# Router and norm of both chunks of the first batch moved into the last attention stage, with five smaller changes

## The reference

```python
x = L0_attn_x                                   # (2, 1024, 128), fp32
x = _layernorm(x + attn(x, qw, kw, vw, ow))     # 16 heads of 8, rope, causal softmax
x = _layernorm(x + ffn(x, router_w, router_b, w1, w3, w2))
# ffn: logits = x @ router_w + router_b ; the best 2 of 4 experts, their probabilities
#      normalised to sum 1 are the gates; expert e: (silu(x @ w1[e]) * (x @ w3[e])) @ w2[e],
#      w1, w3: (4, 128, 512), w2: (4, 512, 128); out = sum of gates * expert
```

## Time and profile before

| | us |
|---|---|
| median of 3 runs | 436.62 (435.84 to 437.49) |
| profiled execution, its time | 432.75 |
| its span | 430.7 |
| busy: PE, DVE, ACT, POOL | 391.1, 315.1, 265.1, 193.5 |
| mean granted TensorE clock | 0.955 |

### The profile page before, as it was taken

One profiled execution on the slowest core, in us unless ns is written; L12 is line 12 of the kernel. 1 busy time (PEld: TensorE's weight loads), 2 busy tenths in 40 slices (PEclk: granted clock), 3 DMA queues, 4 the chain that ended last, 5 costly groups with the idle time before them and its releaser, 6 DMA issues.

```text
span 430.7 us, 7532 instructions
## 1 busy us (share of the span) xinstructions
PE 391.1 (91%) x2420; PEld 202.9 (47%) x2420; DVE 315.1 (73%) x1027; ACT 265.1 (62%) x377; POOL 193.5 (45%) x256
## 2 busy tenths in 40 slices
PE   4658769999999999999999888999999999999991
PEld 2243122232323323233232331788887887888770
DVE  3659888999999999999999543346576658656653
ACT  1233615687786867778687886566665656665550
POOL 7627611261343515235261322466565646655661
PEclk9959686999999999999999998999999999999996
DMA  6474841322213122131210000000000000000000
GB/s 216 153 203 91 286 115 23 75 53 57 52 22 89 39 70 51 25 93 22 74 35 3 1 3 2 0 2 1 2 1 24 2 1 24 2 1 3 24 0 24
DMA packets 45244, 21.13 MB, mean 49 GB/s; under 512 B 30995, under 2 KB 42899, under 8 KB 45206
## 3 DMA queue, kind: packets, MB, share of 16 engines
q1 hardware_dynamic: 44950, 20.47, 18.2%
q10 hardware_dynamic: 256, 0.20, 0.2%
HBM read 13.11 MB, written 7.35 MB: 47 GB/s over the span
## 4 chain that ended last, share of the span: by engine, by line
PE 70%; DVE 9%; ACT 5%; DMA 4%; issue 4%; POOL 3%; SPq 3%; ACTq 0%; POOLq 0%; DVEq 0%
PE o_bank L1127 14%; PE t_bank L1195 9%; PE bank L1084 9%; PE bank L1195 9%; PE t_bank L1206 9%; PE t_bank L1109 8%; PE small_bank L1084 5%; DMA q_op<-max_rows 3%; SPq L442 3%; ACT num L696 2%; DVE num L912 2%; POOL roped L509 1%; DVE num L985 1%; DVE x_w L850 1%; PE o_bank L1214 1%
## 5 line engine op out<-in xcount | busy, mean ns | idle before, releaser
L696 ACT ACTIVATE num<-t_bank 128x1024 f32<-128x1024 f32 (+2 forms) x160 | 142.8, 939 | 60.4 <-PE t_bank L1109 59.7
L610 POOL TENSOR_TENSOR hid_lo<-num,q_op 128x512 fp32r<-128x512 f32 x64 | 83.0, 1300 | 61.2 <-ACT q_op L749 60.0
L574 POOL TENSOR_SCALAR_AFFINE_SELECT num<-num 128x512 f32<-128x512 f32 x64 | 40.1, 636 | 120.7 <-ACT num L696 120.7
L1084 PE MATMUL bank<-k_op,q_op 128*128 128x512 bf16 (+7 forms) x256 | 71.8, 339 | 11.4 <-DMA q_op<-q_scratch 7.1
L1127 PE MATMUL o_bank<-num,v_op 128*32 128x512 f32 (+3 forms) x768 | 81.5, 503 | 0.1
L749 ACT ACTIVATE q_op<-num 128x512 fp32r<-128x512 f32 x64 | 40.5, 632 | 45.0 <-DVE num L985 44.5
L854 DVE TENSOR_REDUCE maxima<-bank 128x1 f32<-128x512 f32 x86 | 57.0, 684 | 2.6 <-PE bank L1084 1.6
L1109 PE MATMUL t_bank<-q_op,k_op 64*128 64x512 bf16 (+3 forms) x384 | 49.6, 337 | 4.3 <-ACTq L677 1.7
L1084 PEld LDWEIGHTS bank<-k_op,q_op 128*128 128x128 bf16 x256 | 21.2, 99 | 63.6 <-DVE maxima L854 23.4
L985 DVE TENSOR_TENSOR num<-bank,num 128x512 f32<-128x512 f32 x32 | 22.1, 691 | 30.7 <-ACT num L756 30.5
L850 DVE CUSTOM_DVE_ANT_0 mg_w<-bank,resid 128x256 f32<-128x256 f32 (+7 forms) x92 | 39.3, 447 | 4.7 <-PE bank L1084 3.8
(11 more groups left out here) (142 smaller groups left out, 629.2 us busy)
## 6 DMA issues: line engine op xcount, KB each, us to landing
q_op<-q_scratch SPq DMA_DIRECT2D x64, 48.0 KB
w_raw<-in_w_all SPq DMA_DIRECT2D x6, 512.0 KB, 4.0
k_op<-k_scratch SPq DMA_DIRECT2D x60, 48.0 KB, 1.9
xT<-in_x_feat SPq DMA_DIRECT2D x4, 256.0 KB, 5.9
q_op<-max_rows SPq DMA_DIRECT2D x64, 3.0 KB
out_tokens<-num SPq DMA_DIRECT2D x4, 256.0 KB, 2.3
q_scratch<-num SPq DMA_DIRECT2D x2, 384.0 KB, 2.8
k_scratch<-num SPq DMA_DIRECT2D x2, 384.0 KB, 2.8
```

The costliest lines, as they stand in the source:

```text
L574: pool.affine_select(out=tile, in_=tile, compare_op=ALU.is_ge, fill=0.0, base=0, pattern=[[0, GH], [1, P]], channel_multiplier=-1)\
L610: pool.tensor_tensor(hid_lo[:, m % HB, :], hid[:, m % HB, :], hid_hi[:, m % HB, :].bitcast(F32), ALU.subtract).then_inc(f_lo, 1)
L696: act.activation(num[:, t % PB, :, off:CH].rearrange("p (k i) t -> p i k t", i=2)[:, :, h:h + each, :], t_bank[k % TB][:, :, 0:each * (CH ...
L1084: ins = pe.matmul(ring(s, step)[:, i * width:(i + 1) * width], q_op[u][:, pr, j, :, :].rearrange("p i q -> p (i q)"), k_op[u][:, pr, lo:lo ...
```

## The change

- **C steps of two chunks in LAST.** There are 22 slots instead of 15; slot i holds r = i of chunk 0 and r = i - 7 of chunk 1. C_AT, the T units behind which they stand, is now 2, 2, 3, 4, 5, 6, 6, 7, 8, 9, 10, 10, 11, ..., 19. Chunk 1 uses PSUM bank 1, chunk 0 bank 0 as before. In these steps the copies of r = 0, 1, 7 and 8 are VectorE's, the store of x1 (r = 9) is GpSimd's, and ScalarE keeps only the tanh. The slots 0 and 1 stand ahead of MROWS(1) in the list, where slot 0 alone stood. Each chunk has its own chain semaphore. Between the experts of chunks 0 and 1 nothing is left of `between`.
- **Experts ahead of the last NORM.** The units 0 and 1 of TensorE's experts stand between the last OCOPY and the last NORM, and wait for the top two of both chunks. The other engines' order is as it was.
- **Rope.** For n = 0 and 1 sum and third part are VectorE's; for n = 4 to 7 the first rest is GpSimd's, inside its P step. Table 0 is loaded by ScalarE's queue.
- **FIRST** has its own string: MROWS(1) behind four S units instead of two, a NORM (of the ones that o_sb[1] is filled with) early, the T units further apart.
- **W2** takes the two products with the high part first and waits for the low part only ahead of the third.
- **C_AT_UNIT** spreads the steps of chunks 2 and 3 over the units: r = 0 at unit 0, nothing at unit 1, r = 1, 2, 3 at units 2, 3, 4, r = 5 to 14 at units 5 to 14.

```diff
@@ -80,7 +80,14 @@
 C_STEPS = 15
-C_AT = [2 + 16 * r // 14 for r in range(C_STEPS)]
+C_LAG = 7
+C_SLOTS = C_STEPS + C_LAG * (NC - 1)
+C_AT = [2 + 17 * i // (C_SLOTS - 1) for i in range(C_SLOTS)]
+def c_steps_of(slot):
+    return [(ch, slot - C_LAG * ch) for ch in range(NC) if 0 <= slot - C_LAG * ch < C_STEPS]
...
         plan.append(("T", c, kt, h, ahead))
-        if not with_s and at in C_AT:
-            plan.append(("C", C_AT.index(at)))
+        plan += [("C", i) for i in range(C_SLOTS) if C_AT[i] == at]
         part = min(1, t_work(t_units[S_LATE:x + 1]) / max(1, t_work(t_units[S_LATE:len(t_units) - S_EARLY])))
         while done_s < len(s_units) and s_work(s_units[:done_s + 1]) <= part * s_work(s_units):
...
                 plan += pv(t)
-        plan.append(("NORM", NC - 1))
+        plan += [("E", 0), ("E", 1), ("NORM", NC - 1)]
...
 STEADY_ORDER = "ssmttssspssttsspssttsspsstspsttssspmsttsssptsspssttssspssttsspssttsspsnttnpp"
+FIRST_ORDER = "ssssmssssnsssststsstsstsssttsspssttsspmsttssspssttsspssttsspssnttppp"
...
 assert [sum(x[0] == k for x in STEADY) for k in ("S", "T", "PV", "MROWS", "NORM")] == [NS, NT, NPV, 2, 2]
-FIRST = steady_plan(STEADY_ORDER.replace("t", "", SEG_T[0] - T_END[0]).replace("p", "", TI), done=TI - 1)
+FIRST = steady_plan(FIRST_ORDER, done=TI - 1)
...
 HEAD = Z_STEP + 1 - UNITS
+C_AT_UNIT = [0, C_STEPS, 1, 2, 3, *range(5, C_STEPS), C_STEPS]
...
+        def load_table(eng, c):
+            cols = slice(c * CH, (c + 1) * CH)
+            eng.dma_start(cos_sb[:, cols], cos_t[:, cols]).then_inc(ld_tab[c], 16)
+            eng.dma_start(sin_sb[:, cols], sin_t[:, cols]).then_inc(ld_tab[c], 16)
         def load_q(eng, n, u, c, heads):
...
                 sp.dma_start(xT[:, ch * CH:(ch + 1) * CH], x_feat[:, ch * CH:(ch + 1) * CH]).then_inc(ld_x[ch], 16)
-                if ch < NC:
-                    cols = slice(ch * CH, (ch + 1) * CH)
-                    sp.dma_start(cos_sb[:, cols], cos_t[:, cols]).then_inc(ld_tab[ch], 16)
-                    sp.dma_start(sin_sb[:, cols], sin_t[:, cols]).then_inc(ld_tab[ch], 16)
+                if ch == 1:
+                    load_table(sp, 1)
...
+            def first_rest(n):
+                pool.wait_ge(part_ready[0], n + 1)
+                pool.tensor_tensor(roped[:, n % 2, :], roped[:, n % 2, :], rope_part(n, 0), ALU.subtract)\
+                    .then_inc(rest_ready, 1)
             def sum_of_turns(n):
                 pool.wait_ge(turned, n + 1)
...
             pool.memset(minus_half[:, :], -0.5).then_inc(ops_filled, 1)
-            sum_of_turns(0)
-            sum_of_turns(1)
             def lay_v(g, b, u):
...
                             third_part(step[1] - 1)
+                        if step[1] < 2 * CHUNKS:
+                            first_rest(step[1])
                     if 0 <= n < GROUPS - 1 and step == ("T", 1, 1, 0, 0):
                         pool.wait_ge(pv_done, PB + NPV * n)
                         lay_v((n + 1) % NG, (n + 1) // NG, u)
                     if step[0] == "C":
-                        between(0, step[1], first=True)
+                        for ch, r in c_steps_of(step[1]):
+                            between(ch, r, first=True)
                     if step[0] != "T":
                         continue
...
-            third_part(0)
-            third_part(1)
             for n in range(2, PROJ_FIRST):
                 sum_of_turns(n)
...
+                if first and r == 9:
+                    pool.wait_ge(c_x1, 1 + ch + 1)
+                    pool.tensor_copy(x1[:, ch * TI:(ch + 1) * TI, :].rearrange("p i d -> p (i d)"), x1_w[:, :])\
+                        .then_inc(c_store, 1)
                 if r == 3:
                     pool.wait_ge(c_var, ch + 1)
...
                     experts(i, n)
-                    between(i + 1, n - HEAD)
+                    if i + 1 >= NC:
+                        between(i + 1, C_AT_UNIT[n - HEAD])
             for n in range(HEAD, Z_STEP + 1):
                 experts(CHUNKS - 1, n)
...
+            load_table(act, 0)
             act.wait_ge(ld_proj, 32)
...
                     if step[0] == "C":
-                        between(0, 0, 0, step[1], first=True)
+                        for ch, r in c_steps_of(step[1]):
+                            if r == 12:
+                                between(ch, 0, ch, r)
             for n in range(-1, GROUPS - 1):
                 stage(STAGES[n + 1], n, split=n > 0)
-            def between(ch, b, c, r, first=False):
-                turns = bank[0] if first else bank[7]
+            def between(ch, b, c, r):
+                turns = bank[7]
                 if r == 0:
-                    act.wait_ge(job_read, SB + (LAST_JOBS if first else NJOBS))
+                    act.wait_ge(job_read, SB + NJOBS)
                     act.wait_ge(c_mgt, 1 + ch)
                     act.activation(mg_w[:, :].rearrange("p (i g r) -> p i g r", i=TI, g=NG),
...
+            def sum_of_turns(n):
+                dve.wait_ge(turned, n + 1)
+                dve.tensor_tensor(roped[:, n % 2, :], by_cos[:, n % 2, :], by_sin[:, n % 2, :], ALU.add)\
+                    .then_inc(roped_ready, 1)
+            def third_part(n):
+                dve.wait_ge(part_ready[1], n + 1)
+                dve.tensor_tensor(rope_part(n, 2), roped[:, n % 2, :], rope_part(n, 1), ALU.subtract)\
+                    .then_inc(part_ready[2], 1)
             turns_of(0)
-            for n in range(1, PROJ_FIRST):
+            sum_of_turns(0)
+            turns_of(1)
+            first_rest(0)
+            sum_of_turns(1)
+            third_part(0)
+            first_rest(1)
+            third_part(1)
+            for n in range(2, PROJ_FIRST):
                 turns_of(n)
-                first_rest(n - 1)
+                if n > 2:
+                    first_rest(n - 1)
             first_rest(PROJ_FIRST - 1)
...
                             turns_of(step[1])
-                        if step[1] > PROJ_FIRST:
-                            first_rest(step[1] - 1)
                     if step[0] == "MROWS":
                         _, c, use = step
...
                     if step[0] == "C":
-                        between(0, step[1], first=True)
+                        for ch, r in c_steps_of(step[1]):
+                            between(ch, r, first=True)
             CHAIN_0, CHAIN = 0, NC
...
-                C_CHAIN = 1 + 2 * TI + 12
-                turns = bank[0] if first else bank[7]
+                turns = bank[ch] if first else bank[7]
                 def then(ins, k):
-                    ins.then_inc(c_step, 1)
-                    dve.wait_ge(c_step, ch * C_CHAIN + k)
+                    ins.then_inc(c_step[ch], 1)
+                    dve.wait_ge(c_step[ch], k)
                 k = 1 + 2 * TI
+                if first and r == 0:
+                    dve.wait_ge(job_read, SB + LAST_JOBS)
+                    dve.wait_ge(c_mgt, 1 + ch)
+                    dve.tensor_copy(mg_w[:, :].rearrange("p (i g r) -> p i g r", i=TI, g=NG),
+                                    merged[:, 1:1 + NG, ch * TI:(ch + 1) * TI, :].rearrange("p g i r -> p i g r")).then_inc(c_mg, 1)
+                if first and r == 1:
+                    dve.wait_ge(c_mgt, 1 + ch + 1)
+                    dve.wait_ge(c_y, 1 + ch)
+                    dve.tensor_copy(mg_t[:, :], turns[:, :]).then_inc(c_mgs, 1)
                 if r == 1:
                     dve.wait_ge(c_y, 1 + ch + 1)
                     then(dve.tensor_tensor(resid[:, :], turns[:, :],
                                            x_res[:, bass.ds(ch * TI, TI), :].rearrange("p i d -> p (i d)"), ALU.add), 1)
                 if r == 2:
-                    statistics(lambda i: resid[:, i * D:(i + 1) * D], c_step)
+                    statistics(lambda i: resid[:, i * D:(i + 1) * D], c_step[ch])
                 if r == 3:
-                    variance(c_step, ch * C_CHAIN + 1, c_var)
+                    variance(c_step[ch], 1, c_var)
                 if r == 5:
                     dve.wait_ge(c_x1t, 1 + ch)
                     dve.wait_ge(c_store, 1 + ch)
                     dve.wait_ge(c_rstd, ch + 1)
                     normalise(lambda i: resid[:, i * D:(i + 1) * D], lambda i: x1_w[:, i * D:(i + 1) * D], c_x1)
+                if first and r == 7:
+                    dve.wait_ge(c_x1t, 1 + ch + 1)
+                    dve.tensor_copy(x1_hi[ch], turns[:, :]).then_inc(c_hi, 1)
                 if r == 7:
                     dve.wait_ge(c_hi, 1 + ch + 1)
                     dve.tensor_tensor(x1_lo[ch], turns[:, :],
@@ -946,6 +998,10 @@
                 upper = tri[:, 0:1, :].broadcast_to([P, TI, E * E])
                 lower = tri[:, 1:2, :].broadcast_to([P, TI, E * E])
                 gt_f, ge_f = (m[:, :, :, :].rearrange("p i e j -> p i (e j)") for m in (gt, ge))
+                if first and r == 8:
+                    dve.wait_ge(c_log, 1 + ch)
+                    dve.wait_ge(c_lo, 1 + ch + 1)
```

(26 more changed lines are left out.)

## The result

The changed kernel takes 447.05 us (median of 4 runs, 445.37 to 447.62) against 436.23 for the kernel before in the same comparison (434.77 to 437.49): ratio 1.024, 95% interval 1.020 to 1.029, so 8.7 to 12.5 us slower. The profiled execution took 447.45 (span 445.6) against 432.75 (430.7). The executions of the kernel before fall into two groups, with spans of 430.4 to 431.7 and of 432.1 to 434.4, and the profiled one is of the lower, so a difference of two spans (14.9 here) can stand 2 to 4 us above one of two medians (10.8). I had forecast 443.0, within 437.2 to 446.8: the direction was right, the size was 4 us short, and the time lies just above the range.

The account below looks back on a forecast made before the run. TensorE, 70% of the chain, was taken to bound the kernel through its instruction stream's waits. Terms summed to +6.4, taking the profiled 432.75 to 439.15; with the median's 3.9 offset, 443.0 us, range 437.2 to 446.8.

Parts of the forecast that it names:

- step 5 of the last stage: Last stage's end: chunk 1's L1182 ends 270.6 to 271.2, then 6.3 of products and T units, last product at 277.6.
- The last stage: Last attention stage with chunk 1's steps and eight copies moved to VectorE: +9.3, bounds +6 and +11.
- E0: Unit 0 of TensorE's experts, behind the last stage; forecast to fill, with unit 1, the 0.71 idle before the last NORM.
- The prologue: Prologue up to the first T unit: GpSimd's added rests delay ScalarE's credit, T unit at 49.4 instead of 47.41, +2.0.
- FIRST: Start of FIRST: VectorE's wait of 1.2 for MROWS(1) vanishes, the one of 0.88 shrinks; -1.3, between 0 and -2.
- Handover: Into the experts: VectorE's last NORM stands before its first hid, which comes at 272.4 instead of 271.71; +0.7 (0 to +1).
- Chunk 1 out of the loop: Experts' loop of chunk 0: chunk 1's four TensorE steps leave it; -2.8 (-2.5 to -3.4).
- W2: Experts: two high-part products fit in the wait of 0.91 for GpSimd's late low part; -0.4 (0 to -0.5).
- Chunks 2 and 3: Experts' loops: the step after the copy one unit later removes two waits of L1171; -1.1 (to +0.6 if crowded).
- The idle of the last stage covers it: Rival: 4.5 us of idle TensorE absorbs the last stage's added work, sum -2.9, time 433.7; chance 0.07.
- Bound by VectorE: Rival: VectorE, not the credit, bounds the prologue, -3.6 instead of +2.0, time 437.4; chance 0.11.
- Longer: Rival: last-stage waits keep the clock at 0.50 and prologue rests take 1.8; +9 to +10, time 446; chance 0.12.

Follow-up runs that it names:

- p_rests_dve: Kernel before plus the change's prologue part, but the rests of n = 4 to 7 stay on VectorE; ratio 0.999 to the kernel before.
- p_table_sp: Kernel before plus the change's prologue part, but table 0 stays on SP's queue; ratio 1.005 to the kernel before.
- p_first: Kernel before plus the whole prologue part, FIRST's new order and W2's order of products; ratio 0.999 to the kernel before.
- norm_first: Kernel before plus FIRST's and W2's orders, one-chunk last stage, n = 0, 1 sums and third parts on VectorE, last NORM ahead of the experts; ratio 0.984.
- cast_first: Kernel after, with last-stage slot 1 one T unit later, so MROWS(1)'s cast precedes chunk 0's second copy and residual; ratio 1.024 to the kernel before.

## Where the prediction was right, and where it failed

The direction and most of the mechanism came as forecast: the gate behind GpSimd's rest of n = 7, VectorE's waits at the start of FIRST gone but for 0.4, the late cast with a gap of 3.0 behind it, the further gaps, and a loop 2.7 shorter. Two terms failed: the steps of chunks 2 and 3, which cost where a gain was forecast, and step 5 of the last stage, whose last 6.3 us were added up at full clock. By its terms the forecast was short by more than the 4.0 of the medians: the sum was +6.4, and the profiled executions differ by 14.9 in span (439.15 forecast, 447.45 measured in time). I had added the 3.9 by which the median stood above the profiled execution before; in the kernel after the profiled execution stands 0.4 above the median. That this hid half of the miss is luck.

**The last stage, +9.3 forecast, +11.6 measured up to the last product with v.** The walk held to 0.2 us for most of the way. With the stage's later start of 2.96 taken off: T(1,0,0) at 251.55 forecast, 251.50 measured; chunk 0's top 265.35, and 265.25; normalise of chunk 1 done 266.55, and 266.7; TensorE's wait before its transposes 2.9, and 2.62; before L1247 2.0, and 2.18. The failing step is number 5, the term "Behind it ... 6.3", which was added up at full clock. Between L1247's start and E0 there are 10.0 us, where I had 0.9 to 1.5 and 6.3. The rows at 272.84 and 274.64 show why: both stand at the 1.2 GHz level behind two waits of 2.6 and 2.2, and the clock of the 6.3 us from 274.70 was 0.71 (0.50 from 272.84 to 278.00, 1.00 from 280.00 on). Against the earlier trace rows the eight small products took 0.8 longer, the eight with v behind them 0.9, the next eight 0.5. TensorE also waits 0.4 for GpSimd's masks there, which I had not counted. I had charged half clock in full once, behind the late rows, where it came (0.58 in the 4.08 us from 254.46), and named "every wait followed by 4 us at 1.2 GHz" as the upper bound, +11. The measured +11.6 lies above that bound, though not every wait was followed so: behind the one of 0.95 at 259.89 the clock was 1.00, and for the first 0.9 us behind the one of 2.62 too. A copy of 512 columns within SBUF took 0.42, below the 0.65 I took and near the 0.35 that I estimated by the Trainium skill (VectorE: DVE Perf Modes, What auto-detection actually checks); whether the chain gained by it no run shows.

**The prologue, +2.0 forecast, +3.3 measured.** The chain on GpSimd was sized well: from the sum of n = 4 to the second part of n = 7 it is 13.5 (37.01 to 50.54), forecast 14.1, with rests of 1.16 (1.20 taken) and sums of 1.27. By the rule on the shared port pair I took 1.27 and no meetings; `p_rests_dve`, where the rests are on VectorE again, has its six sums at 1.46 on average, which agrees. What failed is the start: forecast 35.15, 0.9 earlier than before, and measured 37.01, 0.95 later. I took the table on ScalarE's queue "at nothing", and "0.5 worse if it takes transfer time from x". The first product came at 6.64 instead of 5.89, and so in every kernel with the table there (6.52 to 7.29 in seven, 5.84 to 6.06 in the nine others). But this is not all of the miss: with the table off that queue the score units start 1.1 earlier than before, yet the sum of n = 4 only 0.15 earlier (35.91 against 36.06, `p_table_sp`), so an earlier start of the score units is no earlier start of the gate. And 37.01 is the latest of seven executions with that same start (from 35.83), so up to 1.2 of it is chance.

**FIRST, -1.3 forecast, -0.5 measured**; alone it gives 1.5 in the trace, near the forecast. The terms were added as if independent. The traces say that behind the late prologue they are not; the ratio of `p_first` is what independent terms give, so this stays open.

**Handover, +0.7**: it measured 0.6, and `norm_first` shows it by itself, 0.8. **Chunk 1 out of the loop, -2.8**: -2.7. **W2, -0.4**: the wait went from 0.9 to 0.4.

**Chunks 2 and 3, -1.1 forecast with +0.6 as the bound, +3.1 measured in the kernel after.** The step that failed is "removes the two waits of L1171". They fell to 0.4, and two of 1.8 came. I did not walk that chain to its end: the list keeps normalise in its unit and moves everything before it, which puts the power right ahead of it. The bound of +0.6 came from no row.

Of the 8.5 us between the sum (+6.4) and the spans (+14.9), 4.2 lie in this term, 2.3 in the last stage, 1.3 in the gate and 0.8 in FIRST; the small rest cancels. *The idle of the last stage covers it* was wrong, and the runs show what in it is true: 2.7 of TensorE's 4.5 of idle time there was for ScalarE's copies, and with these on VectorE and one chunk the stretch is 2.9 shorter. *Bound by VectorE* was wrong by the T unit. *Longer*, at 446 with a chance of 0.12, was the nearest to what came; of its two reasons the clock held, and rests at 1.8 did not (1.16).

## What to carry to other kernels

An idle share of an engine is no room for a second chain of round trips: one chunk's chain fit into this stage at no cost and the second, with 3.5 us of TensorE's work, cost 15. When a step in a balanced loop is shifted, walk the whole chain behind it against what GpSimd does in the same microseconds, above all for VectorE's operations that read and write SBUF alone. And behind a wait of 2 to 3 us forecast TensorE's next microseconds at 1.2 GHz, and do not keep that for the bound: it was 0.58 over 4.08 us behind the wait of 3.0, and 0.50 over 5.2 us behind those of 2.6 and 2.2. A change of many parts is to be taken apart: here two parts give about 3 us each by themselves (the orders of FIRST and W2; the last stage of one chunk with its copies on VectorE), and four cost, by the traces, 3.3 (prologue; 2.7 by its ratio), 3.1 (chunks 2 and 3; 4.2 by its ratio), 0.8 (handover; too small for the times) and 12.4 (chunk 1 in the last stage; 9.4 by the ratios).

## What the runs showed beyond that

Taking a wait away shortened the stage by less than the wait where the granted clock fell in its place (`cast_first`: 3.3 us less idle, clock 0.88 to 0.83, stretch 1.4 shorter). Two transfers of 256 KB on ScalarE's queue (cos and sin, 3.1 and 3.8 us to landing) delayed TensorE's first product, which waits for loads on SP's queue, by 0.75, although nothing uses the two until 10.5. And kernels that are the same program up to GpSimd's sum of n = 4 came to it at 35.83 to 37.01: a single pair of traces does not tell half a microsecond from chance, while the chain from there to the first T unit took 11.4 in every kernel with the rests on VectorE and 13.7 in every one with them on GpSimd.
